# Two 16-head attentions: scores made twice, in one-pass products on four row groups, instead of scores, transposes and evacuations

## What is computed

```
q = norm(x) Wq + bq          # 128 x 128, 16 heads of 8 columns
k = ctx Wk + bk ; v = ctx Wv + bv
s_h = q_h k_h^T / sqrt(8)    # per head 128 x 128
p_h = softmax(s_h)           # the first attention masks some keys
x = x + tanh(g) * (concat_h(p_h v_h) Wo + bo)
```

## Time and profile before

| | us |
|---|---|
| device time, median of 3 runs | 591.96 (591.91 to 594.07) |
| the profiled execution's own time | 594.07 |
| its span in the trace | 594.0 |
| first 16-head attention, scores to last add | 28.1 to 91.1 |
| second 16-head attention, scores to last add | 375.6 to 437.6 |

### The profile page before, as it was taken

The page is one execution under the profiler, slowest core; times in us unless marked ns, Lnnn a source line. Parts: engine busy times, 40 slices in busy tenths (PEclk is TensorE's granted clock), DMA queues, the critical chain, the costliest instruction groups (busy, mean ns, idle before and its releaser), DMA issues.

```text
span 594.0 us, 10687 instructions
## 1 busy us (share of the span) xinstructions
PE 566.0 (95%) x3685; PEld 410.5 (69%) x3689; DVE 381.8 (64%) x736; ACT 384.2 (65%) x781; POOL 243.2 (41%) x229
## 2 busy tenths in 40 slices
PE   8999998999999997999799999999999999999997
PEld 6567766787664775777555556577668788888885
DVE  1678865756741647777454666478838666666665
ACT  4277776755666447888675656677875566666663
POOL 5006673485014100111015681000024788888884
PEclk8999998999989999999989999999999999999999
DMA  8300001161000000000000102000001666666650
GB/s 253 144 2 2 2 1 33 20 168 47 7 2 1 0 1 1 1 2 1 2 0 1 40 14 67 1 2 1 2 5 42 163 171 174 184 173 180 183 132 35
DMA packets 14850, 33.54 MB, mean 56 GB/s; under 512 B 2912, under 2 KB 8432, under 8 KB 14672
## 3 DMA queue, kind: packets, MB, share of 16 engines
q1 hardware_dynamic: 14800, 32.89, 19.5%
HBM read 32.03 MB, written 0.85 MB: 55 GB/s over the span
## 4 chain that ended last, share of the span: by engine, by line
PE 76%; DVE 8%; ACT 7%; issue 6%; POOL 2%; DMA 1%; ACTq 0%; DVEq 0%; SPq 0%; POOLq 0%
PE bank L845 9%; PE bank L847 9%; PE bank L846 9%; PE bank L728 5%; PE bank L739 5%; PE bank L754 3%; PE bank L687 3%; ACT wa L1418 2%; PE bank L702 2%; PE bank L650 2%; PE bank L644 2%; PE bank L1253 2%; PE bank L1128 2%; PE bank L1142 2%; PE bank L1117 1%
## 5 line engine op out<-in xcount | busy, mean ns | idle before, releaser
L504 POOL TENSOR_TENSOR h_lo<-wc,h_hi 128x512 fp32r<-128x512 f32 x54 | 70.0, 1300 | 13.7 <-ACT h_hi L1487 13.7
L845 PE MATMUL bank<-xn_hi,w_hi 128*128 128x512 f32 x168 | 66.0, 393 | 3.4 <-DVE xn_lo L1975 3.1
L847 PE MATMUL bank<-xn_hi,w_lo 128*128 128x512 f32 x168 | 65.4, 390 | 0.0
L846 PE MATMUL bank<-xn_lo,w_hi 128*128 128x512 f32 x168 | 65.4, 389 | 0.0
L1964 DVE TENSOR_TENSOR wb<-arena,bank 128x512 f32<-128x512 f32 x64 | 44.0, 687 | 33.0 <-PE bank L847 33.0
L1487 ACT ACTIVATE h_hi<-wc 128x512 fp32r<-128x512 f32 x54 | 34.0, 633 | 37.6 <-DVE wc L1972 27.9
L496 POOL TENSOR_TENSOR w_lo<-ring,w_hi 128x384 fp32r<-128x384 f32 x42 | 42.7, 1019 | 19.1 <-ACT w_hi L1464 19.1
L1746 DVE TENSOR_TENSOR wa<-bank,row_max 128x512 f32<-128x512 f32 x64 | 44.3, 691 | 7.5 <-ACT wb L1364 4.3
L1364 ACT ACTIVATE wb<-wa 128x512 f32<-128x512 f32 x64 | 40.1, 630 | 13.7 <-DVE wa L1746 13.3
L1742 DVE TENSOR_REDUCE row_max<-bank 128x4 f32<-128x512 f32 x64 | 43.6, 682 | 5.9 <-PE bank L728 5.4
L1370 ACT ACTIVATE wc<-bank 128x512 f32<-128x512 f32 x64 | 38.0, 593 | 8.4 <-PE bank L739 7.8
(11 more groups left out here) (351 smaller groups left out, 1392.2 us busy)
## 6 DMA issues: line engine op xcount, KB each, us to landing
arena<-comb_rows SPq DMA_DIRECT2D x64, 256.0 KB, 4.1
ring<-in_experts SPq DMA_DIRECT2D x42, 192.0 KB, 2.5
ring<-in_experts SPq DMA_DIRECT2D x8, 256.0 KB, 4.0
mats<-in_mats SPq DMA_DIRECT2D x1, 1472.0 KB, 10.5
mats<-in_mats SPq DMA_DIRECT2D x1, 832.0 KB, 6.7
mats<-in_mats SPq DMA_DIRECT2D x2, 320.0 KB, 8.2
x<-in_x_t SPq DMA_DIRECT2D x1, 512.0 KB, 4.7
context<-in_ctx_t SPq DMA_DIRECT2D x1, 512.0 KB, 5.0
```

The source lines that it names most:

```text
L504: nc.gpsimd.tensor_tensor(h_lo[:, v % 3, :], hidden_of(v), h_hi[:, v % 3, :].bitcast(f32), ALU.subtract).then_inc(m_h_lo, 1)
L845: mm(out, w, x_, start=start, stop=False)
L846: mm(out, w, x_rest, start=False, stop=False)
L847: return mm(out, w_rest, x_, start=False, stop=stop)
```

## The change

Scores are made twice, both times by one-pass products (fp32r) on all four row groups. So that one pass is as exact as fp32, each k and each q row is split into a rounded part and a rest, and the 32 rows of a head hold three blocks of eight: the spread weights are copied three times, and DVE subtracts the rounded part where a column `rest_cols` says so (L1830 and L1831 in the new file; four late k splits of the first attention go to POOL, L600 and L603; four late q splits per attention go into DVE's loop, L1847). The first copy of the scores (L779) serves the maxima only: DVE reduces two banks at a time, 1024 columns, into `top_wide` (L1860), PE turns that (L793), and DVE adds the negative maxima to four further rows of the q rows (L1866). The second copy (L805) exchanges the operands, so that the scores come out already turned and less their maximum; ACT takes the exponential straight from two banks of PSUM, 1024 columns (L1462), and the result feeds the products with the values (L825). Transposes, subtraction and evacuation of the probabilities are gone. Scores of batch b go to two of three pairs of banks in turn, two batches ahead. The tail is spread over four batches: turn of o (L837) for b-2, turn back (L858) for b-3, projection (L847) for b-4. The splits of the second attention's k rows stand in the mixture of 8 experts, two before its norm, two after it, four in the expert loop; those of its q rows just before it. The maxima of the fake-quantised weights move from ahead of the first attention into DVE's loop there. POOL's adds and fake-quantise steps stand as before.

The core of the diff:

```diff
@@ TensorE
-                def scores(b, p):
+                def scores(b):
...
                     if b > 0:
-                        pe.wait_ge(a_sub, base + 4 * b + 2 * p - 2)
+                        pe.wait_ge(a_max, 2 * (tb + b))
+                    if b >= 2:
+                        pe.wait_ge(a_exp, 2 * (tb + b - 2) + 1)
                     for m_ in range(QUADS):
-                        for i in range(2):
-                            r = 2 * p + i
+                        for r in range(4):
                             rows = slice(32 * r, 32 * r + 32)
-                            ins = mm(bank[r][:, m_ * P:m_ * P + P], q_rows[rows, m_, b * P:b * P + P],
+                            ins = mm(bank[score_bank(b, r)][:, m_ * P:m_ * P + P], q_rows[rows, m_, b * P:b * P + P],
                                      k_rows[rows, m_, b * P:b * P + P], start=True, stop=True)
...
-                def transposes(b, u):
...
+                def turn_tops(b):
+
+                    pe.wait_ge(a_max, 2 * (tb + b) + 2)
...
+                    nc.tensor.transpose(bank[7][:, 2 * P:3 * P], top_wide[:, :], ident[:, :]).then_inc(a_top, 1)
...
+                def turned_scores(b):
+
+                    pe.wait_ge(a_taken, tb + b + 1)
+                    if b > 0:
+                        pe.wait_ge(a_exp, 2 * (tb + b))
+                    if b + 1 < B:
+                        pe.wait_ge(a_max, 2 * (tb + b + 1) + 1)
                     for m_ in range(QUADS):
...
+                            ins = mm(bank[score_bank(b, r)][:, m_ * P:m_ * P + P], k_rows[rows, m_, b * P:b * P + P],
+                                     q_rows[rows, m_, b * P:b * P + P], start=True, stop=True)
...
+                scores(0)
                 q_rows_of(inst, 1)
...
+                turn_tops(0)
+                scores(1)
                 for b in range(B):
...
+                    turned_scores(b)
+                    if b >= 2:
+                        turn_o(b - 2)
+                    if b + 1 < B:
+                        turn_tops(b + 1)
+                    if b >= 4:
+                        through_o(b - 4)
+                    if b >= 3:
+                        turn_back(b - 3)
+                    if b + 2 < B:
+                        scores(b + 2)
+                    if b >= 1:
+                        probs_v(b - 1)
@@ ScalarE
+                def exp(b, p):
+                    act.wait_ge(a_st, 2 * (tb + b) + p + 1)
+                    if b >= 2:
+                        act.wait_ge(a_pv, tb + b - 1)
+                    at = score_bank(b, 2 * p)
+                    fn(probs_of(b, p), banks[:, at:at + 2, :], ACT.Exp, scale=SCALE_A).then_inc(a_exp, 1)
@@ VectorE
+            def rows_split(dst, raw, rounded, rests, done):
+
+                link(v.tensor_scalar(rounded.bitcast(f32r), raw, rest_cols[:, rests - 1:rests], None, ALU.mult))
+                v.tensor_tensor(dst, raw, rounded, ALU.subtract).then_inc(done, 1)
...
+                def largest(b, p):
+                    dve.wait_ge(a_s, 2 * (tb + b) + p + 1)
...
+                    v.tensor_reduce(tops, banks[:, at:at + 2, :].rearrange("p r (m k) -> p r m k", m=QUADS), X, ALU.max)\
+                        .then_inc(a_max, 1)
+
+                def take_tops(b):
+                    dve.wait_ge(a_top, tb + b + 1)
+                    part = q_rows[:, :, b * P:b * P + P]
+                    v.tensor_tensor(part, bank[7][:, 2 * P:3 * P].unsqueeze(1).to_broadcast([P, QUADS, P]),
+                                    part.bitcast(f32), ALU.add).then_inc(a_taken, 1)
...
+                for b in range(B):
+                    if b + 1 < B:
+                        take_tops(b + 1)
+                    if b >= 2:
+                        divide(b - 2)
+                    if b < 2:
+                        q_rows_late(inst, 2 * b)
+                        q_rows_late(inst, 2 * b + 1)
+                    if b + 2 < B:
+                        largest(b + 2, 0)
+                        largest(b + 2, 1)
+                    beside(b)
...
+            for n in range(2):
+                k_rows_split(1, n)
             norm(NORM_OF[5][0])
+            for n in range(2, 4):
+                k_rows_split(1, n)
...
+                if k in LATE_KEYS:
+                    k_rows_split(1, 4 + LATE_KEYS.index(k))
@@ GpSimd
+            for n in range(4, 8):
+                pool.wait_ge(a_k_raw, n + 1)
+                nc.gpsimd.tensor_scalar(late_round[:, n % 2, :].bitcast(f32r), k_raw(0, n),
+                                        rest_cols[:, K_REST - 1:K_REST], None, ALU.mult).then_inc(a_k_round, 1)
```

More of the change, by code:

```diff
@@ L142, in flamingo_kernel @@
         comb_pieces2 = comb_pieces[:, :, 0:64].bitcast(bf16)
-        bank = [ctx.enter_context(nc.psum_tensor(f"bank{n}", [P, 512], f32)) for n in range(8)]
+        banks = ctx.enter_context(nc.psum_tensor("bank", [P, 8, 512], f32))
+        bank = [banks[:, n, :] for n in range(8)]
         in_ident, in_ctx, in_x, in_mask, in_consts, in_mats1, in_mats2, in_mats3 = (
@@ L1546, in _ @@
             norm_rest(0)
-            for c in range(2):
-                act.wait_ge(a_mask_rows, c + 1)
-                fn(mask_rows[:, c, :], bank[5 + c][:, :], ACT.Copy).then_inc(a_mask_out, 1)
+            act.wait_ge(a_bias_rows, 1)
+            k_rows_out(0, 0, bank[4])
             act.wait_ge(in_mask, 32)
@@ L1552, in _ @@
             nc.scalar.preload_act_table(ACT.Exp)
-            act.wait_ge(a_bias_rows, 1)
+            for n in range(1, 4):
+                k_rows_out(0, n, bank[4 + n % 3])
             q_rows_out(0, 0)
+            for n in range(4, 8):
+                k_rows_out(0, n, bank[4 + n % 3])
             act.wait_ge(pool_ready, 6)
@@ L2196, in _ @@
             norm(NORM_OF[6][0])
-            attn(1)
+            for n in range(4):
+                q_rows_split(1, n)
+            attn(1, lambda b: None)
             norm(NORM_OF[7][0])
```

423 lines of the change are left out of this document (236 added, 187 removed).

## The result

The changed kernel takes 597.16 us (596.63 to 598.38), the kernel before 591.97: a ratio of 1.0084, with a 95% interval of 1.0063 to 1.0104. It is slower, by more than half a per cent, and the forecast was 585.1 and faster.

The account below looks back on a forecast made before the run. TensorE (PE) was taken to set the attentions' pace. First attention +1.4, routing +3.0, expert loop +2.0 and second attention -13.3 took the profiled 594.07 to 587.2, less 2.1 for a median: 585.1 us, range 576 to 598.0.

Parts of the forecast that it names:

- Row groups and maxima: Attention loop: 16 one-pass scores on four row groups take .6 us, two 1024-column maxima 2.35, a batch 4.1 against 6.76.
- The first rival: Attention scores: four row groups run no faster than two, 5.1 us a batch, 597.5 us in all; chance .15.
- Nor is PE with 3.4, as long as its clock is at full speed: Attention loop: PE needs 3.4 us of a 4.1 us batch, so it is not the bound at full clock.
- The clock rival: Both attentions: PE pauses in every batch, its clock falls and PE is the bound again, 588 to 602 us; chance .10.
- two of the signs that the forecast had named: Profile after: score groups over 1.1 us or a granted clock of 0.5 inside an attention would show the forecast wrong.
- Second attention, -13.3: Second 16-head attention: shrinks from 62.20 to 48.9 us, a gain of 13.3.
- This attention's gain is lost to POOL: First attention: POOL's 31.3 us start with a first add at 58.6, so it ends at 91.5 against 91.1.
- Norm behind it, +1.0: Norm after the first attention: about 3 us at the lower clock level, a third on the path, +1.0 (bounds 0 and 5).
- Routing, +3.0: Top-2 MoE routing: two k splits on DVE between normed x and first maximum cost +3.0 us (bounds 1.9 and 4.5).
- Expert loop, +2.0: Expert loop of the top-2 MoE: four k splits on DVE at .5 us each, +2.0 (bounds 0 and 8).
- The second rival: Routing and expert loop: POOL stretches a split to 3.1 us, +3.4 and +2 to 4, giving 589 to 593; chance .13.
- the first op of a split: Splits on DVE: first op taken as .55 us from the rows; the skill page gave an estimated .4.

Follow-up runs that it names:

- f2_warm: Changed kernel plus idle TensorE products in both attentions' heads and first four batches: 593.0 us, ratio .9993 to the kernel before.
- f3_quant: Changed kernel with weights' maxima back ahead of the first attention and 8 of 20 fake-quantise steps before POOL's first add: 590.55 us, ratio .993.
- f4_all: Changed kernel with the edits of f2_warm and f3_quant, and six k splits of the second attention moved into DVE's gaps: 572.55 us, ratio .9655.
- f1_before: The kernel before, unchanged, run once more for a second trace: 594.05 us; its profiled execution 595.25 for a span of 593.4.
- h1_old5: Changed kernel with only the five idle products put back that the change dropped from each attention's head: 598.31 us, ratio 1.0075.
- e1_warm: Changed kernel plus idle products where PE waits in both attentions' heads, fewer than in f2_warm: 595.07 us, ratio .9974.
- g1_before_quant: The kernel before with only POOL's order of adds and fake-quantise steps changed as in f3_quant: 592.97 us, ratio .9993.

## Why the prediction was wrong, by its own steps

- *Row groups and maxima: right.* A group of 16 scores takes .67 where .6 was taken, two maxima 2.35 as worked out (1.13 and 1.22), a batch 3.92 where 4.1 was forecast, all at the full clock. The first rival (four row groups no faster than two) is refuted by the same rows; that the measured 597.16 lies next to its 597.5, and inside the range, is chance. The .6 was partly luck as well: its row of 32 in 1.72 is two halves in a row, each on two row groups (the order of the code for batch 0), so it did not show four groups side by side. The products with the values take 1.08, under the 1.15 to 1.7 given for them, and 4 x 1.24 less 3 x .91 is 2.2 where 2.3 stands; neither matters.
- *"Nor is PE with 3.4, as long as its clock is at full speed": the step that failed.* The condition did not hold. The clock rival, given .10, is what happened, in its partial form: at the lower level for some four batches of each attention (20.5 us), with two of the signs that the forecast had named, score groups over 1.1 and a granted clock of 0.50 inside an attention. f2_warm measures it: 4.6 us in the second attention (59.9 against 55.3), 3.4 in the first (78.8 against 75.3), 8.0 of the 11.4 us by which the forecast was off. The rival looked for the cause in the pauses of the loop; the runs put it in the head and the first batches, where the forecast had worked out the idle time of PE itself (8.45 us with some 5.3 of products in them, and 2.6 ahead of it) and had drawn no conclusion for the clock. The loop at full level keeps its level with its pauses (8.60 of 10.30 us busy, 418.20 to 428.50); with the longer ones that POOL's pace makes in the first attention it does not (0.84, 60.48 to 93.70).
- The Trainium skill, "TensorE: Matmul & The Clock Gate", section "A second HAM failure mode: psum-queue depth-cycling", led to that rival. The trace agrees that a PE with pauses can lose its level. It does not agree that the level swings from group to group: it stayed at 0.50 for 20.5 us at a stretch, and at 1.00 from 418.20 on, in one loop through the same banks.
- *Second attention, -13.3: size off.* Measured -7.3. 4.6 of the difference is the clock, and 1.4 the rest: at the full level the gain was 11.9.
- *"This attention's gain is lost to POOL": right, and its mechanism exactly so.* First add at 58.6 forecast, 60.48 measured; end 91.5 forecast, 93.70 measured; POOL's chain 32.9 and 33.2. The end lies 2.2 later: the clock put the first add 3.5 later (57.01 in f2_warm), and without that it would have come 1.6 ahead of the forecast. The forecast took POOL as given; f3_quant and f4_all show that its order, not its work, was the bound.
- *Norm behind it, +1.0:* +1.4. The middle stages moved by +.7. Both are within what the two traces of the kernel before differ by, so neither is shown.
- *Routing, +3.0:* +1.9, at the lower end of its bounds.
- *Expert loop, +2.0: the term that was mis-sized.* +4.5, inside the bounds of 0 and 8. Each split was priced at .5. What counted was that a split stands ahead of the next tokens' scaling: PE's waits for it went from .6 to 4.5 us. The second rival had the stretch (3.1 at worst; 2.1 to 2.6 measured, above the 2 that the forecast had named as a sign); the forecast named the place ("behind each split waits the next gather's result") and gave the wait almost no price. "DVE has room" was true of its busy share (29.90 of 46.00 us) and false of the place.
- On the stretch the Trainium skill has a rule that the forecast did not use, in "SBUF — State Buffer", section "Who interferes with whom": an op with two inputs in SBUF contends with a GpSimd instruction that reads SBUF, an op by a scalar can contend with GpSimd when it runs in a two-port mode, and an op with at most one SBUF input outside these modes does not. The rows agree: L1830, L1831 and L2298 come stretched (1.22, 1.10, 1.89) beside POOL, while L2283 and L2290, which read PSUM for one of their tensors, stay at .73 and .67.
- On the first op of a split, the Trainium skill, "VectorE: DVE Perf Modes", section "The perf-mode tier table", led to an estimate of .4, the rows before to .55. Measured without POOL: .48.

Together: forecast -6.9, measured +4.5 by stages against f1_before. Of the 11.4 between them the second attention has 6.0, the first 2.9, the loop 2.5, the norm and the middle stages 1.1, and the routing gave back 1.1.

What stays open: the traced execution of f3_quant stayed at the lower level longer than the changed kernel in both attentions, that of h1_old5 longer in the second and shorter in the first, and e1_warm lost its level in the first attention in spite of its idle products (3.95 of 5.00 us busy ahead of the fall). Just when the level falls and when it comes back is not settled by these runs, only that it fell behind the thin heads (1.94 of 5.00 us busy) and did not behind the filled ones of f2_warm and f4_all (4.82 of 5.00).

## What to carry to other kernels

Work taken off the engine that sets the pace is won only where something else lets the next stage start: before counting a gain, follow the adds, copies and steps in program order behind it on the engine that was idle so far. When a change thins out TensorE, price its heads and waits for the clock as carefully as its products, and fill them first. Work that moves to an engine with room has to land in that engine's gap, on the far side of what others wait for.

## What the runs showed of the hardware that was not expected

- One loop ran at either clock level, and the busy share of PE hardly told them apart: 17.37 of 20.50 us and 17.26 of 20.48 at 0.50, 8.60 of 10.30 at 1.00.
- A reduction across partitions on POOL takes .37 us, but in f3_quant POOL stood idle, by "issue", for 5.76 us ahead of it and 7.13 behind, between its ordinary tile ops:

```profile
42.67 0.37 POOL L606 PARTITION_ALL_REDUCE w_max<-w_max  x1 [5.76 <-issue]
50.18 1.58 POOL L571 TENSOR_SCALAR diag<-mats,w_stat 128x512 f32<-128x512 f32 x1 [7.13 <-issue]
```

The five other runs of the changed kernel with the steps right behind the reduction have the same gaps (5.5 to 5.9 ahead, 7.0 to 7.5 behind), and g1_before_quant has 7.09 behind it. What POOL does in them, no trace shows. In the kernel before, and in the changed one, POOL had nothing to do around the reduction, and such a gap could not show.
